# One head's reciprocal and scaling, moved to earlier places in VectorE's program

## The chip, the cores and the metric

The kernel runs on one core of a Trainium2 chip. The metric is the device time of one execution in microseconds (us). Engines are called PE (TensorE, matmuls), DVE (VectorE), ACT (ScalarE), POOL (GpSimd) and SP (SyncE, which here only issues DMAs). Each engine works through its own program in order, and they meet at semaphores.

## The reference

Two transformer-like layers over x of shape (4, 1024, 256). Layer 0 is a long convolution and an FFN with binarized weights; layer 1 is causal attention with 16 query heads on 4 key heads and a mixture-of-experts FFN. The change touches the attention alone:

```python
q = (hidden_states @ Wq).reshape(b, s, H, D).transpose(0, 2, 1, 3)      # H = 16, D = 64, s = 1024
k = (hidden_states @ Wk).reshape(b, s, HKV, D).transpose(0, 2, 1, 3)    # HKV = 4
v = (hidden_states @ Wv).reshape(b, s, HKV, D).transpose(0, 2, 1, 3)
q = _apply_rope(q, cos, sin)
k = _apply_rope(k, cos, sin)
scores = jnp.einsum('bkgqd,bkpd->bkgqp', qg, k) * scale
scores = jnp.where(causal, scores, jnp.float32(-1e+30))
probs = jax.nn.softmax(scores, axis=-1)
out = jnp.einsum('bkgqp,bkpd->bkgqd', probs, v).reshape(b, H, s, D)
return out.transpose(0, 2, 1, 3).reshape(b, s, H * D) @ Wo
```

The softmax of a head divides by a sum for each query. The kernel does this last: it multiplies the head's 64 x 1024 output by the inverse sums.

## The kernel before

A loop runs over the four batches. Inside it the layers follow each other; the attention is a loop over 16 heads (u, one "turn" each), and each turn over 12 blocks (n = 0 to 11) of the causal score matrix, 128 keys by up to 512 queries: 4 blocks for the first 512 queries, 8 for the second. The order of the work on each engine is written out by hand, and all that an engine does for a turn hangs on n:

- PE, block n: the scores of the block (`score_cols`), then score rows of the next head for its maxima (`score_rows`, one of 8 row tiles, at the n of `ROWS_AT`), at n = 8 the transposition of the maxima (`turn_maxima`), and the product with the values of the block four back (`values`). Scores go to six PSUM banks used in rotation. In turns 4 and 8 (and 0) PE also projects queries of a later key group at n = 4.
- ACT, block n: exp of the scores twice, to a full and a rounded copy (`exps`). Behind block 4 it copies out the second half of the previous head's output with its sums (`summed(u - 1, 1)`), behind block 8 the first half of this head's; behind block 9 it copies the next head's maxima (`turn_maxima`).
- POOL: masks of diagonal blocks, and the low part (full minus rounded) of blocks 0 to 5.
- DVE, block n: row maxima of the next head (`row_maxima`, tiles 0 and 1 at n = 0, then one tile for each n up to 6), their negation at n = 6 (`negate`), the low part of blocks 6 to 11 (`score_low`), and two small steps that finish an earlier head:
  - `invert(u)` waits for head u's sums in `den` and takes their reciprocals, 128 x 8, into `rden`;
  - `scale(u)` waits for the reciprocals spread over 64 partitions in `rb` (a part of the tile `mix`) and multiplies `osum` (in the tile `work`) by them into `oT`, 64 x 1024.
- SP, turn u, in this order: queries for later heads; `load_sums(u - 1)` (`den` from `osum`, issued once ACT has copied the sums); `load_maxima(u + 1)` (issued once ACT has copied the maxima); `spread_inverse(u - 1)`, which waits for the reciprocals, stores them to memory, waits for the store and loads them as a broadcast into `rb`; and in turns 0, 4, 8 the store of rotated rows to `q_scratch`, with a second one a turn later.

SP's part of a turn reads:

```python
                    if u:
                        load_sums(u - 1)
                    if u + 1 < HEADS:
                        load_maxima(u + 1)
                    if u:
                        spread_inverse(u - 1)
```

PE's first scores of a turn wait for the maxima that `load_maxima` brings, and ACT overwrites a head's half of `osum` two turns later, once its scaling is done.

Of the kernel before, what the change touches and what calls it, by code (L numbers as in the profile page):

```python
# [35 lines left out]
HEADS, KV, HD = 16, 4, 64  # L36
# [59 lines left out]
def adaln_hyena_binffn_gqa_moe(nc, d, out, gate_scratch, kf_scratch, q_scratch, k_scratch, inverse_scratch, scratch):  # L96
    es = ExitStack()
    with es:
# [792 lines left out]
        def _(dve):  # L891
# [131 lines left out]
            def rotate(k):  # L1023

                cols = slice(0, HALF) if (k % 2 if k >= 4 else k // 2) == 0 else slice(HALF, L)
                for e in range(2):
                    b = bk.wait(dve, ("rope", k, e))
                    V.tensor_tensor(turned(k)[:, 2 * e:2 * e + 2, :], ps[:, b, :].unsqueeze(1).broadcast_to([P, 2, HALF]),
                                    rope[:, :, cols], ALU.mult).then_inc(s["rope_a"], 1)
# [9 lines left out]
            def low(k):  # L1039

                dve.wait_ge(s["rope_hi"], k + 1)
                V.tensor_tensor(split_of(k)[:, 1], turned(k)[:, 0:2, :], split_of(k)[:, 0].bitcast(F32), ALU.subtract)\
                    .then_inc(s["rope_lo"], 1)

            def row_maxima(u, i):
                n = (i + 1) * P
                b = bk.wait(dve, ("rows", u, i))
                v = (ps[:, b:b + 2, :].rearrange("p a n -> p (a n)") if n > HALF else ps[:, b, :])[:, 0:n]
                V.tensor_tensor_reduce(out=v, in0=v, in1=mrow[:, L - n:L], scale=1.0, scalar=-3e38, op0=ALU.add,  # L1049
                                       op1=ALU.max, accum_out=mx[:, u % 2, i:i + 1]).then_inc(freed[b], 1)  # L1050

            def negate(u):
                dve.drain()
                V.tensor_scalar(nm[:, u % 2, :], mx[:, u % 2, :], -1.0, None, ALU.mult).then_inc(s["nm_done"], 1)
# [11 lines left out]
            def score_low(u, c, j):  # L1066
                if j * P >= c * HALF:
                    dve.wait_ge(s["masked_done"], NT * u + j + 1)
                else:
                    dve.wait_ge(s["exp_done"], NBLK * u + 4 * c + j + 1)  # L1070
                n, m = NBLK * u + 4 * c + j, HALF - max(0, j * P - c * HALF)
                V.tensor_tensor(plo[:, n % PRING, 0:m], full(n)[:, 0:m], phi[:, n % PRING, 0:m].bitcast(F32), ALU.subtract)\  # L1072
                    .then_inc(s["low_dve"], 1)

            def invert(u):
                dve.wait_ge(s["sum_loaded"], 16 * (u + 1))
                if u >= 2:
                    dve.wait_ge(s["inverse_stored"], 16 * (u - 1))
                V.reciprocal(rden[:, u % 2, :], den[:, u % 2, :]).then_inc(s["inverse_done"], 1)

            def scale(u):
                dve.wait_ge(s["inverse_loaded"], 16 * (u + 1))
                V.tensor_tensor(oT[u % 2 * HD:(u % 2 + 1) * HD, u // 2, :], osum[0:HD, u % 2, :], rb[:, :], ALU.mult)\
                    .then_inc(s["oT_done"], 1)
# [12 lines left out]
            with dve.Fori(0, B) as bi:  # L1097
# [3 lines left out]
                for n, e in enumerate(E_ORDER):  # L1101
                    dst = tapped(e)
                    b = bk.wait(dve, ("up", n, 1)) - 1
                    u = ps[:, b:b + 2, :].rearrange("p a n -> p (a n)")
# [91 lines left out]
                for u in range(HEADS):  # L1196
                    w = u + 1
                    k = 2 * GROUP_AT[u] + 2 if u in GROUP_AT else None
                    for n, blk in enumerate(BLOCKS):
                        if n == 4 and k and u:  # L1200
                            rotate(k)
                            rotate(k + 1)
                        if w < HEADS:
                            for i in ROWS_AT.get(n, ()):
                                row_maxima(w, i)
                        if n == 9 and u:
                            invert(u - 1)
                        if n == 6 and w < HEADS:
                            if w >= 2:
                                dve.wait_ge(s["nmr_done"], w - 1)  # L1210
                            negate(w)
                        if n == 7 and k:
                            low(k)
                        if blk in DVE_LOW:
                            score_low(u, *blk)
                        if n == 2 and u >= 2:
                            scale(u - 2)
                    if k:
                        low(k + 1)
                scale(HEADS - 2)  # L1220
                invert(HEADS - 1)
                scale(HEADS - 1)
                add_to_x("out1", 0, gates[:, 2, :])
# [410 lines left out]
```

## Time and profile before

| | |
|---|---|
| median of 3 runs | 2246.38 us (2244.85 to 2249.71) |
| the profiled execution | 2244.85 us, span in the profile 2243.0 us |
| busy over the span | PE 81%, DVE 68%, ACT 44%, POOL 47% |
| mean granted PE clock | 0.92 |
| attention turns of the first batch, 256 to 550 us | of 294 us: PE busy 248.58, DVE 195.34, ACT 183.23, POOL 201.09 |
| DVE's waits for the broadcast reciprocals | 53.3 us in 24 places |
| PE's waits for the maxima of a turn | 37.7 us in 56 places |

Busy times are those of an engine's own instructions; the rest of a line is idle. Times within the execution are counted from the start of the span. The share of busy time says little here; what counts is which wait ends last at each step of a turn.

### The profile page before, as it was taken

To read this page: it belongs to the slowest core of one execution; us is meant where nothing else is said; L and a number is where in the kernel's file an instruction comes from. 1 tells how busy PE (TensorE), PEld (TensorE's weight loads), DVE (VectorE), ACT (ScalarE), POOL (GpSimd) and SP (SyncE) were. 2 spreads that over 40 slices of the span, in tenths; PEclk is the share of its full clock that TensorE was granted. 3 is DMA by queue.
4 is the path that set the end of the run, shared out by engine and by line. 5 is a ranking of instruction groups with operands and counts; after the bars stand their busy time and mean duration, and the time that the engine had idled before them with its cause. 6 is when DMAs were issued, how large, how long until landed. Compare 5 with 4: busy or idle time off the path is not lost.

```text
span 2243.0 us, 27366 instructions
## 1 busy us (share of the span) xinstructions
PE 1808.7 (81%) x8596; PEld 1379.2 (61%) x8596; DVE 1533.7 (68%) x2838; ACT 996.5 (44%) x2113; POOL 1057.9 (47%) x1699
## 2 busy tenths in 40 slices
PE   6868788888866888878876878888887687978897
PEld 4657565566755666656665765665576475656666
DVE  4597866665668867666458886666555887766745
ACT  1303365565322345656331336556722043665643
POOL 0151366675133147667315127677722413766741
PEclk9989899999988889999988889999998898999999
DMA  5400433331410134332150043343141005333304
GB/s 223 178 1 1 113 102 97 90 88 33 169 49 1 49 98 108 91 95 67 30 202 1 1 113 90 78 109 89 35 174 54 1 1 146 90 95 81 85 25 188
DMA packets 92203, 187.26 MB, mean 83 GB/s; under 512 B 29119, under 2 KB 44287, under 8 KB 88326
## 3 DMA queue, kind: packets, MB, share of 16 engines
q1 hardware_dynamic: 84742, 171.66, 26.3%
q10 hardware_dynamic: 7296, 13.63, 2.1%
q8 instruction: 76, 1.25, 0.2%
q14 instruction: 89, 0.73, 0.1%
HBM read 129.39 MB, written 45.89 MB: 78 GB/s over the span
## 4 chain that ended last, share of the span: by engine, by line
PE 39%; DVE 16%; POOL 13%; DMA 10%; issue 8%; ACT 6%; DVEq 5%; SPq 1%; POOLq 1%; ACTq 0%
PE ps L367 7%; POOL plo L1316 6%; PE ps L663 5%; PE ps L490 5%; DMA q<-nmr 4%; PE ps L373 3%; DVE ps L1049 3%; DMA q_scratch<-hrow 3%; ACT phi L785 3%; PE ps L704 3%; PE ps L528 3%; PE ps L510 3%; PE ps L529 3%; PE ps L531 3%; POOL pT L1307 2%
## 5 line engine op out<-in xcount | busy, mean ns | idle before, releaser
L1049 DVE CUSTOM_DVE_ANT_0 ps<-ps,mrow 128x128 f32<-128x128 f32 (+7 forms) x512 | 384.0, 772 | 161.0 <-PE ps L490 160.7
L784 ACT ACTIVATE pT<-ps 128x512 f32<-128x512 f32 (+3 forms) x512 | 257.6, 503 | 286.8 <-POOL plo L1316 146.4
L785 ACT ACTIVATE phi<-ps 128x512 fp32r<-128x512 f32 (+3 forms) x768 | 377.6, 492 | 0.0
L1305 POOL TENSOR_SCALAR_AFFINE_SELECT phi<-phi 128x128 fp32r<-128x128 f32 x512 | 174.3, 340 | 404.9 <-ACT phi L785 400.5
L490 PE MATMUL ps<-khl,qhh 128*128 128x512 f32 (+3 forms) x768 | 241.5, 388 | 130.0 <-ACT phi L785 100.8
L510 PE MATMUL ps<-qhh,khl 128*128 128x512 f32 (+3 forms) x768 | 280.4, 365 | 50.6 <-DMA q<-nmr 37.7
L1316 POOL TENSOR_TENSOR plo<-pT,phi 128x512 fp32r<-128x512 f32 (+2 forms) x256 | 272.5, 1075 | 16.0
L511 PE MATMUL ps<-q,k 65*128 65x512 f32 (+3 forms) x768 | 272.1, 354 | 0.0
L528 PE MATMUL ps<-phi,vhi 128*65 128x512 f32 (+3 forms) x768 | 267.7, 349 | 2.0 <-POOL pT L1307 1.8
L531 PE MATMUL ps<-plo,vhi 128*65 128x512 f32 (+3 forms) x768 | 265.4, 346 | 4.2 <-POOL plo L1316 3.0
L529 PE MATMUL ps<-phi,vlo 128*65 128x512 f32 (+3 forms) x768 | 263.9, 344 | 0.0
L490 PEld LDWEIGHTS ps<-khl,qhh 128*128 128x128 f32 x768 | 139.9, 207 | 192.3 <-ACT phi L785 137.8
L1271 POOL TENSOR_TENSOR rstd<-var,neghalf 128x4 f32<-128x4 f32 x34 | 34.5, 1015 | 432.4 <-DVE var L961 432.4
L510 PEld LDWEIGHTS ps<-qhh,khl 128*128 128x128 f32 x768 | 149.5, 195 | 129.6 <-ACT phi L785 49.1
L1072 DVE TENSOR_TENSOR plo<-pT,phi 128x512 fp32r<-128x512 f32 (+2 forms) x256 | 156.3, 627 | 93.3 <-POOL pT L1307 64.5
L743 ACT ACTIVATE work<-ps,modb 128x512 f32<-128x512 f32 x48 | 37.3, 777 | 401.4 <-PE ps L445 401.4
L511 PEld LDWEIGHTS ps<-q,k 65*128 65x128 f32 x768 | 149.6, 195 | 12.6
L784 ACT ACTIVATE mix<-ps 128x512 f32<-128x512 f32 (+2 forms) x256 | 120.3, 470 | 60.3 <-PE ps L511 43.8
L531 PEld LDWEIGHTS ps<-plo,vhi 128*65 128x65 f32 x768 | 107.3, 140 | 57.6 <-POOL plo L1316 10.6
L367 PE MATMUL ps<-hT,wqkv 128*128 128x512 f32 x480 | 126.1, 422 | 18.9 <-DVE hT L973 18.9
L1316 POOL TENSOR_TENSOR plo<-mix,phi 128x256 fp32r<-128x256 f32 (+1 forms) x128 | 129.0, 1008 | 10.3 <-ACT phi L785 4.9
L1307 POOL TENSOR_SCALAR_AFFINE_SELECT pT<-pT 128x128 f32<-128x128 f32 x320 | 130.3, 407 | 0.0
(177 smaller groups left out, 3520.6 us busy)
## 6 DMA issues: line engine op xcount, KB each, us to landing
qhh<-q_scratch SPq DMA_DIRECT2D x112, 256.0 KB, 5.1
q_scratch<-hrow SPq DMA_DIRECT2D x24, 1024.0 KB, 5.5
mix<-inverse_scratch SPq DMA_DIRECT2D x64, 256.0 KB, 3.5
q<-q_scratch SPq DMA_DIRECT2D x56, 256.0 KB, 4.4
sgn<-sgn_scratch SPq DMA_DIRECT2D x8, 1024.0 KB, 13.6
Kf<-kf_scratch SPq DMA_DIRECT2D x4, 2048.0 KB, 17.3
khl<-k_scratch SPq DMA_DIRECT2D x24, 256.0 KB, 5.9
in_w<-in_w_scratch SPq DMA_DIRECT2D x4, 1536.0 KB, 10.8
```

The source lines that it names most:

```text
L367: i = mm(o, lhs(a, q), rhs(c, q), start=n == 0, stop=n == len(pairs) - 1)
L490: q = mm(ps[:, b + c // HALF, 0:e - c], qhh[:, r, i * P:(i + 1) * P], khl[:, g % 2, c:e], start=True, stop=True)
L510: mm(ps[:, b, 0:hi - lo], khl[:, g % 2, j * P:(j + 1) * P], qhh[:, r, lo:hi], start=True, stop=False)
L511: mm(ps[:, b, 0:hi - lo], k2[:, g % 2, j * P:(j + 1) * P], q2[:, u % 2, lo:hi], start=False, stop=True)\
L528: mm(o, vhi[:, g, j, :], high, start=j == 0, stop=False)
L529: mm(o, vlo[:, g, j, :], high, start=False, stop=False)
L531: mm(o, vhi[:, g, j, :], low, start=False, stop=j == 4 * c + 3).then_inc(s["pv_done"], 1)
L784: A(full(n)[:, 0:hi - lo], ps[:, b, 0:hi - lo], ACT.Exp, scale=SCALE)
L785: A(phi[:, n % PRING, 0:hi - lo], ps[:, b, 0:hi - lo], ACT.Exp, scale=SCALE)\
L1049: V.tensor_tensor_reduce(out=v, in0=v, in1=mrow[:, L - n:L], scale=1.0, scalar=-3e38, op0=ALU.add, op1=ALU.max, accum_out=mx[:, u % 2, i:i ...
L1307: G.affine_select(out=v, in_=v, compare_op=ALU.is_ge, fill=0.0, base=0, pattern=[[1, P]], channel_multiplier=-1).then_inc(s["masked_done"], 1)
L1316: G.tensor_tensor(plo[:, n % PRING, 0:m], full(n)[:, 0:m], phi[:, n % PRING, 0:m].bitcast(F32), ALU.subtract)\
```

## The change

In turn u, DVE takes the reciprocals of head u - 1 at block 4 instead of block 9, in front of the low parts, and scales head u - 1 at block 9 of the same turn, behind block 9's low part. Before, it scaled head u - 2 at block 2 of turn u. Head 14's scaling, which stood behind the loop, is thereby inside it. Nothing else is changed: the other engines' programs, SP's among them, are the same.

```diff
@@ -1203,7 +1203,7 @@
                         if w < HEADS:
                             for i in ROWS_AT.get(n, ()):
                                 row_maxima(w, i)
-                        if n == 9 and u:
+                        if n == 4 and u:
                             invert(u - 1)
                         if n == 6 and w < HEADS:
                             if w >= 2:
@@ -1213,11 +1213,10 @@
                             low(k)
                         if blk in DVE_LOW:
                             score_low(u, *blk)
-                        if n == 2 and u >= 2:
-                            scale(u - 2)
+                        if n == 9 and u:
+                            scale(u - 1)
                     if k:
                         low(k + 1)
-                scale(HEADS - 2)
                 invert(HEADS - 1)
                 scale(HEADS - 1)
                 add_to_x("out1", 0, gates[:, 2, :])
```

## Rows read from the trace of the kernel before

**Rows 1.** Windows: length, busy us (instructions) PE, PEld, DVE, ACT, POOL, clock, DMA.

```profile
392.15:408.23 16.08, 14.08 (x74) 9.84 (x74) 11.06 (x26) 11.05 (x27) 11.67 (x23) 1.00 0.30 67
...
356.00:358.00 2.00, 0.00 (x0) 0.00 (x0) 0.00 (x0) 0.00 (x0) 0.00 (x0) 1.00 1.05 394
...
360.00:362.00 2.00, 0.07 (x1) 0.07 (x1) 1.06 (x1) 2.00 (x4) 0.05 (x1) 0.50 0.93 199
```

**Rows 2.** Timeline of SP, heads 6 and 7: start us, us, engine line op out<-in.

```profile
390.20 0.69 SPq L1484 DMA_DIRECT2D q<-nmr  x1
390.93 0.44 SPq L1496 DMA_DIRECT2D inverse_scratch<-rden  x1
392.45 0.49 SPq L1500 DMA_DIRECT2D mix<-inverse_scratch  x1
...
400.28 0.52 SPq L1490 DMA_DIRECT2D den<-work  x1
406.28 0.69 SPq L1484 DMA_DIRECT2D q<-nmr  x1
```

**Rows 3.** Timeline of DVE, head 7; in brackets the idle time before.

```profile
390.70 0.56 DVE L1072 TENSOR_TENSOR plo<-pT,phi 128x384 fp32r<-128x384 f32 x1 [0.40 <-POOL pT L1307]
...
396.12 1.22 DVE L1083 TENSOR_TENSOR oT<-work,mix 64x1024 f32<-64x1024 f32 x1
...
400.54 1.10 DVE L1049 CUSTOM_DVE_ANT_0 ps<-ps,mrow 128x896 f32<-128x896 f32 x1 [1.41 <-PE ps L490]
...
406.18 0.20 DVE L1079 RECIPROCAL rden<-den 128x8 f32<-128x8 f32 x1
```

**Rows 4.** Timeline of PE, head 7: blocks 4 and 7, and the transposition.

```profile
396.19 0.45 PE L510 MATMUL ps<-qhh,khl 128*128 128x512 f32 x1
...
402.20 0.39 PE L510 MATMUL ps<-qhh,khl 128*128 128x512 f32 x1
...
403.75 0.27 PE L497 MATMUL ps<-ident,nm 128*8 128x128 f32 x1 [0.22 <-DVE nm L1054]
```

**Rows 5.** Timeline of ACT, head 7: block 4, the sums, the maxima.

```profile
398.69 0.60 ACT L784 ACTIVATE pT<-ps 128x512 f32<-128x512 f32 x1 [2.18 <-POOL plo L1316]
...
399.66 0.59 ACT L792 ACTIVATE work<-ps 65x512 f32<-65x512 f32 x1
...
406.00 0.25 ACT L771 ACTIVATE nmr<-ps 8x128 fp32r<-8x128 f32 x1
```

**Rows 6.** Tile `den`: landing of all 64 loads, from their issue.

```profile
DMA to landing us min/median/max: 2.0/2.7/4.7
```

**Rows 7.** Tile `mix`, 256 to 556 us: landing of SP's 16 broadcast loads.

```profile
DMA to landing us min/median/max: 3.3/3.5/4.0
```

**Rows 8.** Windows of DVE alone: length, busy us (instructions), clock, DMA share, GB/s.

```profile
391.60:392.70 1.10, 0.78 (x2) 1.00 0.07 4
392.90:394.95 2.05, 1.35 (x6) 1.00 0.58 160
```

**Rows 9.** Timeline of POOL, head 7: the second mask of block 1, block 3's.

```profile
396.15 1.35 POOL L1307 TENSOR_SCALAR_AFFINE_SELECT pT<-pT 128x128 f32<-128x128 f32 x1
...
400.07 0.29 POOL L1307 TENSOR_SCALAR_AFFINE_SELECT pT<-pT 128x128 f32<-128x128 f32 x1
```

**Rows 10.** The critical path behind head 4's turn: start us, us, what.

```profile
351.92 1.39 DMA inverse_scratch<-rden
...
353.86 5.91 DMA q_scratch<-hrow
```

**Rows 11.** Timeline of SP, heads 4 and 15.

```profile
350.17 0.69 SPq L1484 DMA_DIRECT2D q<-nmr  x1
...
541.35 0.51 SPq L1490 DMA_DIRECT2D den<-work  x1
```

**Rows 12.** Timeline of DVE, head 15: the low part of its last block.

```profile
549.01 0.29 DVE L1072 TENSOR_TENSOR plo<-mix,phi 128x128 fp32r<-128x128 f32 x1 [0.19 <-POOL mix L1307]
```

**Rows 13.** The critical path behind head 15's turn.

```profile
549.63 20.54 PE ps L663 x94
```

## The prediction

> **What bounds the kernel now.** I read the page first: the span is 2243.0 us. The critical path and PE's waits then put the disputed code in the attention part, which is 16 turns (one per head) in each of four batches. I took one ordinary turn, head u = 7, from its first score matmul at 392.15 us to the next turn's at 408.23, and laid the engines' timelines side by side. In those 16.08 us PE is busy 14.08, DVE 11.06, ACT 11.05 and POOL 11.67, with PE's clock granted in full [rows 1]. No engine is full. The turn is a loop of dependences, and the question is what the moved waits do to that loop.
>
> With blocks 0 to 11 of a turn, the loop is as follows. SP sends the row maxima of the next head (390.20); the first score matmul follows at 392.15. The exp of block 4 starts at 398.69, the maximum of row tile 6 runs at 400.54, the score matmul of block 7 is at 402.20 and the turning of the maxima at 403.75, ACT copies them out at 406.00, and SP sends the next ones at 406.28 [rows 2, 3, 4, 5]. 390.20 to 406.28 is the 16.08 us again.
>
> The slack around this loop is small. Block 7's score matmul takes the PSUM bank of tile 6, whose maximum ends at 400.54 + 1.10 = 401.64, 0.56 us before the matmul starts. Block 4's score matmul (396.19) has its bank from row tile 2. The exp of block 4 waits 2.18 us for POOL, so that matmul has slack: its first half takes 0.45 us and its second about as much less an overlap, so it ends near 396.9, and could end 1.8 us later for nothing [rows 3, 4, 5].
>
> **The reciprocal, moved from block 9 to block 4.** It needs the sums that SP loads. SP can issue this load only after ACT has copied the sums, which comes right behind block 4's exp: the copy starts at 399.66 and the load is issued at 400.28 [rows 2, 5]. Landing takes 2.7 us from issue in the median of 64, 2.0 to 4.7 at the ends [rows 6]. So the sums are there at 400.28 + 2.7 = 402.98. In the old order DVE reaches the reciprocal at 406.18 and doesn't wait. In the new order it reaches it behind tile 5's maximum, at 400.54 less the 1.41 us of idle time ahead of tile 6, 399.13, and everything behind it waits until 402.98, plus 0.2 for the reciprocal less 0.1 of overlap: 403.1. Behind it stand the maxima of tiles 6 and 7, the negation, and the low parts of blocks 6 to 11. Tile 6 starts at 403.1 instead of 400.54, so block 7's score matmul can't start before about 404.25 instead of 402.20. That is 2.56 us less the 0.56 of slack, and I take 2.1 (by the negation, whose slack is smaller, it is 2.2). From the exp of block 7 to the copy of the maxima ACT works without a pause, so the next SP send is late by the same 2.1 us. Nothing takes this back later in the loop.
>
> SP gains nothing from the earlier reciprocal in an ordinary turn. Its queue holds the send of the maxima (406.28) ahead of the store of the reciprocals, which goes right behind it (390.20 and 390.93); the reciprocal, at 406.18 in this turn, is in time for that already [rows 2, 3].
>
> **The scaling, moved from block 2 two turns behind the head's own to block 9 one turn behind.** Its factors come by a store (SP waits for its landing, from 390.93 to 392.45: 1.5 us) [rows 2] and a broadcast load (3.5 us in the median, 3.3 to 4.0) [rows 7]. The load is issued at 392.45, so the factors land at 395.95 [rows 2, 7], wherever the scaling stands in DVE's program; today the scaling starts at 396.12. In the new order DVE comes to it behind block 9's low part, which ends at 390.70 + 0.56 = 391.26. It then waits 4.7 us. Behind it now stand the low parts of blocks 10 and 11 and the maxima of tiles 0 to 3, which used that time before [rows 3, 8]. From 395.95: scaling 1.22, the two low parts 0.78, the maxima of tiles 0 to 2 with their read-outs 1.35 [rows 3, 8], less some 0.35 for overlaps (my estimate: each instruction starts up to 0.1 before the last one's end, and the last read-out needn't be waited for). That is 3.0, so tile 2's bank is free near 398.95, and block 4's score matmul goes from 396.19 to 399.0, 2.8 us later. On the way PE waits for block 10's low part. Its own exp moves from 398.69 to about 399.7: of the 2.8 us, 1.8 are covered by what it waited for POOL, and 1.0 us is left. The sums are then copied 1.0 us later, and the second wait stands behind them: 1.0 + 2.1 = 3.1 us per turn.
>
> One row makes the scaling cost more than its 1.22 us today: a mask of POOL takes 1.35 us beside it at 396.15 instead of 0.29, which lies on the loop [rows 9]. In the new order the scaling starts at the same moment, so this 1.06 us stays. The Trainium skill (SBUF — State Buffer, Who interferes with whom) has a DVE instruction with two SBUF inputs and a GpSimd instruction that reads SBUF shut each other out, the first one keeping the read port to its end. By that rule the low parts of blocks 10 and 11, which now run right behind the scaling, may hold POOL up to 0.8 us longer; that would fit in what the exp of block 4 waits for PE by then, and changes no term.
>
> **Turns that differ.** Heads 4 and 8 carry the projection of a later group at block 4 on PE. There the reciprocal stands behind four rotations on DVE and its sums have landed, so the first wait costs nothing. The projection sits directly behind block 4's score matmul, so here all 2.8 us pass. In return the reciprocal is no longer late. In these turns SP waits for it: the store at 351.92 has its trigger there, and the store of the rotated rows behind it, at 353.86 and 5.91 us long, is on the critical path [rows 10]. The earlier reciprocal lets SP go on right behind its send (350.17, and 0.73 as in the ordinary turn: 350.90), 1.0 us sooner [rows 2, 11]. Net 1.8 us per such turn. After heads 4 and 8 ACT stands still for that 5.91 us, so DVE's wait for the factors is hidden; heads 5 and 9, like head 1, pay only the first wait.
>
> Head 15 has no maxima to find. The load of its predecessor's sums is issued at 541.35 [rows 11] and lands at about 544.05, before the low parts are urgent. Store, load and scaling then take 1.5 + 3.5 + 1.22 from 544.3, to about 550.4, and the low parts of blocks 10 and 11, now behind it, end near 551.1 instead of 549.01 + 0.29 = 549.30. That is 1.8 us on the last value matmuls [rows 12]. Taking one scaling out of the end saves nothing: PE goes into the output projection without a pause, and is still in it when the last scaling is done (its projection matmuls follow each other for 20.54 us) [rows 13].
>
> **The sum, per batch.** Heads 2, 3, 6, 7 and 10 to 14: 9 x 3.1 = 27.9. Heads 1, 5, 9: 3 x 2.1 = 6.3. Heads 4, 8: 2 x 1.8 = 3.6. End: 1.8. Together 39.6 us, times four batches 158. The profiled execution took 2244.85 us (1.5 below the median of 2246.38 of the three runs), so the forecast is 2403 us.
>
> The unknown prices are the two landings. If every load of sums took 2.0 us, 12 turns a batch would be 0.7 cheaper each: 34 us less, 2369. If each took 4.7, 2.0 dearer each, 96 us more, 2499; since the median is near the short end, I take the middle of 2.7 and 4.7 as a mean that could be, 48 us more, 2451, and with the factors at 4.0 the upper end is 2473. The load of factors at 3.3 instead of 3.5 saves 0.2 x 11 x 4 = 9 us, at 4.0 it costs 22.
>
> The Trainium skill (DMA: Bandwidth & Descriptors, Anatomy of one DMA — SWDGE (gpsimd) path) gives about 2.0 us for any transfer plus bytes over 436 GB/s, and puts nearly all of it on the receipt of the write. It speaks against the change, since a 4 KB load then isn't quick: my estimate by its figures is 2.0 us for the sums, which would give the 2369 above but for the factors' path (4.6 us for store and load, where the rows have 5.0).
>
> **The rivals.**
> - *Only one wait shows.* The 1.0 us that I let pass at block 4 rests on a cover of 1.8 us that I read from one turn. If DVE and PE catch up fully, 9 turns cost 2.1 instead of 3.1 and heads 4 and 8 about nothing: 12 x 2.1 + 1.8 = 27 a batch, 2353 us. For it: DVE idles 16.08 - 11.06 = 5 us in a turn [rows 1]. Against it: that idle time is spread over waits for PE and POOL, and a chain that is late arrives late at each of them. Chance 0.14.
> - *Faster: the factors are there in time.* If SP had stored and loaded them before DVE comes to block 9, the scaling would run in a hole of DVE and would no longer stretch POOL's mask, which is on the loop: 1.06 us x 13 turns x 4 = 55 us less, 2190 us. It decides at one point: the factors must land before 391.3. For it: the reciprocal is ready 5 us earlier. Against it: SP's send of the maxima stands ahead of the store and goes at 390.20 [rows 2]. Chance 0.05.
> - *No change*, the waits all lying beside POOL's work: 2245 us. It needs 2.5 us of slack at tile 6, and the rows show 0.56. Chance 0.04.
> - *More: PE's clock.* PE gets holes of about 2.3 us (at block 10) and 2 us (before block 7) in a turn. The granted clock was full in this turn; should it fall to its lower level (1.2 GHz instead of 2.4) for some 4 us of each turn, and half of the doubled matmul time lie on the loop, that is 1 us x 15 x 4 = 60 us more, 2463 us, up to twice that. Against it: behind head 4's turn PE does nothing from 356 to 358 us at full clock, and only later, at 360 to 362, is it at 0.50 [rows 1]. Chance 0.09.
>
> **How the numbers follow.** The forecast as worked out has 0.68; its own range is 2360 (both short) to 2473. With the first rival's 0.14 the range reaches down to 2345, and with half of the clock's up to 2480. Faster by over 0.2% (about what a measurement of this kernel tells from no change) 0.05, within it 0.04, slower 0.91.
>
> **What would show it.** In the new profile: the scaling preceded by about 4.7 us of idle DVE, released by the load of the factors; a wait of 2.6 to 3.9 us before the reciprocal, put down to the load of the sums; SP's sends of the maxima 19.2 us apart in ordinary turns instead of 16.08; about 2 us of PE waiting for a row maximum before block 7's score. The mask of POOL beside the scaling should still take over 1 us. I am wrong if the sends stay near 16 us apart, if the load of the sums is issued before block 4's exp, or if the clock differs.

## The result, and the profile after

The changed kernel takes 2454.32 us in the median of 4 runs (2449.18 to 2458.99), the kernel before 2245.61 on the same chip: a ratio of 1.0925, 95% interval 1.0899 to 1.0953. It is slower by 209 us, where 158 were forecast. The profiled execution took 2463.96 us with a span of 2462.2, 219 above that of before.

These are the busy times on the two pages, the kernel before first. DVE, ACT and POOL are busy for less time than before or for as long. PE is busy for 116 us more with the same 8596 matmuls: its mean granted clock is 0.88 (0.92 before). In the first batch the attention of the changed kernel runs from about 256 to 612 us at a clock of 0.88; in the kernel before it ran from 256 to 550 us at 0.96.

```profile
PE 1808.7 (81%) x8596; PEld 1379.2 (61%) x8596; DVE 1533.7 (68%) x2838; ACT 996.5 (44%) x2113; POOL 1057.9 (47%) x1699
PE 1925.0 (78%) x8596; PEld 1467.6 (60%) x8596; DVE 1505.9 (61%) x2838; ACT 995.2 (40%) x2113; POOL 998.3 (41%) x1699
```

Read the waits next. These are rows of the changed kernel's waits (engine, line, releaser, us in total, times, longest).

```profile
DVE oT L1083 <- DMA mix<-inverse_scratch: 272.7, 62, 5.5
ACT pT L784 <- DVE plo L1072: 186.3, 48, 4.5
DVE rden L1079 <- DMA den<-work: 163.2, 56, 6.2
...
PE ps L531 <- DVE plo L1072: 115.4, 52, 2.9
...
PE ps L510 <- DVE mx L1049: 44.0, 34, 2.2
```

The first and third are the two waits of the change: 4.4 us each in 62 places, 2.9 us each in 56. The second is a surprise: ACT, 48 times, waits for a low part that DVE makes. Waits add up to more than the loss, because several engines wait for one thing. The chain says which of them set the end. Here it is for one whole ordinary turn of the changed kernel, head 7, from one send of the maxima to the next (start us, us, what):

```profile
411.88 0.69 SPq L1483
...
412.61 1.50 DMA inverse_scratch<-rden
414.13 3.61 DMA mix<-inverse_scratch
417.76 1.22 DVE oT L1083
...
419.01 0.44 DVE plo L1072
...
419.94 0.49 ACT phi L785
...
420.49 0.29 POOL phi L1304
420.79 0.26 POOL pT L1306
...
421.12 1.02 POOL plo L1315
...
422.24 0.60 ACT pT L784
...
423.33 0.49 ACT work L792
423.83 1.96 DMA den<-work
425.82 0.20 DVE rden L1079
...
427.12 0.50 PE ps L510
...
429.73 0.43 PE ps L531
...
431.70 0.15 ACT nmr L771
431.86 0.69 SPq L1483
```

The turn takes 431.86 - 411.88 = 19.98 us instead of 16.08 [rows 2]. For its first 5.8 us nothing computes on the chain: the send, the store, the broadcast load. Then come the scaling, block 10's low part, block 1's exp and its work on POOL, and block 4's exp; the copy of the sums, their load, the reciprocal, and block 7's scores behind tile 6's maximum.

DVE's timeline of the changed kernel has the same in its own rows, with the idle time ahead in brackets:

```profile
417.76 1.22 DVE L1083 TENSOR_TENSOR oT<-work,mix 64x1024 f32<-64x1024 f32 x1 [4.84 <-DMA mix<-inverse_scratch]
419.01 0.43 DVE L1072 TENSOR_TENSOR plo<-pT,phi 128x256 fp32r<-128x256 f32 x1
...
425.82 0.20 DVE L1079 RECIPROCAL rden<-den 128x8 f32<-128x8 f32 x1 [2.61 <-DMA den<-work]
425.94 1.07 DVE L1049 CUSTOM_DVE_ANT_0 ps<-ps,mrow 128x896 f32<-128x896 f32 x1
```

The scaling waits 4.84 us, the reciprocal 2.61. Windows of the changed kernel, with the columns of [rows 1], show the clock behind the second hole of PE: 0.74, then 0.50.

```profile
428.00:430.00 2.00, 1.89 (x8) 0.99 (x8) 1.62 (x5) 2.00 (x5) 0.00 (x0) 0.74 0.02 4
430.00:432.00 2.00, 2.00 (x7) 1.41 (x6) 0.69 (x1) 1.43 (x4) 0.77 (x3) 0.50 0.00 0
```

A good ruler for all kernels here is the time between SP's sends of the maxima, read from the start times in SP's timeline. The first batch (turns 0 to 14; "next" is from the last send to the next batch's first):

```text
turn                 0     1     2     3     4     5     6     7     8     9    10    11    12    13    14   next
before           21.79 19.41 16.03 15.88 20.12 24.00 16.03 16.08 20.10 23.94 16.20 16.07 16.01 16.07 16.34 264.51
after            21.79 21.56 20.60 20.39 24.71 24.23 20.75 19.98 26.13 25.77 20.19 20.09 21.58 19.75 21.38 267.46
e1_scale_only    21.78 20.42 17.58 19.23 25.96 23.29 19.22 20.20 26.07 23.24 18.82 20.56 20.09 20.36 20.80 272.91
e8 (e1, filled)  21.81 19.43 17.80 20.18 25.01 23.27 17.68 17.85 23.18 23.38 17.83 18.00 18.17 17.86 18.06 273.24
e2_invert_only   21.78 21.33 21.50 18.78 20.15 24.42 22.02 17.53 20.11 26.17 21.23 17.77 19.84 17.74 19.72 262.63
e6_spread_first  21.79 23.65 17.71 17.91 20.13 20.64 18.39 17.15 20.24 20.92 17.35 16.52 17.94 16.50 17.00 262.43
e7_both_free     21.78 19.99 15.44 15.26 20.28 20.42 15.48 15.28 22.79 19.66 16.03 17.10 15.27 15.26 15.69 263.84
```

Over four batches the mean difference of after and before is, for turns 2, 3, 6, 7 and 10 to 14, 39.1 us together (4.3 each); for 4 and 8, 5.2 and 5.9; for 1, 5 and 9, 1.9, -0.2 and 0.5; for the rest of a batch 2.3. That is 54.7 us a batch, 219 in four: the whole loss of the profiled execution.

### The profile page after: what moved, and what is told of

Same layout as the page of the kernel before. It is cut to its first block, busy times and chain, and to the rows that moved or that the text cites. A ratio compares the mean times of both kernels' runs of the same rounds, so it can differ in the third digit from the quotient of the medians.

```text
span 2462.2 us, 27366 instructions
## 1 busy us (share of the span) xinstructions
PE 1925.0 (78%) x8596; PEld 1467.6 (60%) x8596; DVE 1505.9 (61%) x2838; ACT 995.2 (40%) x2113; POOL 998.3 (41%) x1699
## 4 chain that ended last, share of the span: by engine, by line
PE 35%; DMA 21%; DVE 17%; issue 6%; ACT 6%; DVEq 5%; POOL 5%; SPq 2%; ACTq 1%; POOLq 1%
DMA mix<-inverse_scratch 8%; PE ps L367 6%; PE ps L663 5%; DMA den<-work 5%; DMA inverse_scratch<-rden 4%; PE ps L510 3%; PE ps L490 3%; PE ps L373 3%; DMA q_scratch<-hrow 3%; PE ps L511 3%; ACT phi L785 2%; PE ps L531 2%; PE ps L704 2%; DVE oT L1083 2%; PE ps L528 2%
## 5 line engine op out<-in xcount | busy, mean ns | idle before, releaser
L531 PE MATMUL ps<-plo,vhi 128*65 128x512 f32 (+3 forms) x768 | 283.4, 369 | 115.8 <-DVE plo L1072 115.4
L510 PE MATMUL ps<-qhh,khl 128*128 128x512 f32 (+3 forms) x768 | 307.1, 400 | 82.1 <-DVE mx L1049 44.0
L490 PE MATMUL ps<-khl,qhh 128*128 128x512 f32 (+3 forms) x768 | 258.8, 414 | 99.8 <-ACT phi L785 67.8
L511 PE MATMUL ps<-q,k 65*128 65x512 f32 (+3 forms) x768 | 292.7, 381 | 0.0
L528 PE MATMUL ps<-phi,vhi 128*65 128x512 f32 (+3 forms) x768 | 286.0, 372 | 0.0
L529 PE MATMUL ps<-phi,vlo 128*65 128x512 f32 (+3 forms) x768 | 280.8, 366 | 0.0
L1315 POOL TENSOR_TENSOR plo<-pT,phi 128x512 fp32r<-128x512 f32 (+2 forms) x256 | 255.3, 1008 | 16.0
L490 PEld LDWEIGHTS ps<-khl,qhh 128*128 128x128 f32 x768 | 161.5, 229 | 154.7 <-ACT phi L785 81.9
L1083 DVE TENSOR_TENSOR oT<-work,mix 64x1024 f32<-64x1024 f32 x64 | 78.9, 1233 | 272.9 <-DMA mix<-inverse_scratch 272.7
L511 PEld LDWEIGHTS ps<-q,k 65*128 65x128 f32 x768 | 164.1, 214 | 17.4
## 6 DMA issues: line engine op xcount, KB each, us to landing
Kf<-kf_scratch SPq DMA_DIRECT2D x4, 2048.0 KB, 17.6
```

Of the source, the lines that this page charges most:

```text
L490: q = mm(ps[:, b + c // HALF, 0:e - c], qhh[:, r, i * P:(i + 1) * P], khl[:, g % 2, c:e], start=True, stop=True)
L510: mm(ps[:, b, 0:hi - lo], khl[:, g % 2, j * P:(j + 1) * P], qhh[:, r, lo:hi], start=True, stop=False)
L511: mm(ps[:, b, 0:hi - lo], k2[:, g % 2, j * P:(j + 1) * P], q2[:, u % 2, lo:hi], start=False, stop=True)\
L528: mm(o, vhi[:, g, j, :], high, start=j == 0, stop=False)
L529: mm(o, vlo[:, g, j, :], high, start=False, stop=False)
L531: mm(o, vhi[:, g, j, :], low, start=False, stop=j == 4 * c + 3).then_inc(s["pv_done"], 1)
```

## The experiments

Times are medians; ratios are to the kernel before, run beside, with a 95% interval. The diffs are against the changed kernel unless said.

**Each part alone.** The two moves were made one at a time. e1_scale_only leaves the reciprocal at block 9:

```diff
-                        if n == 4 and u:
+                        if n == 9 and u:
                             invert(u - 1)
```

> The scaling alone stands in its new place (block 9 of the next turn); the reciprocal stays at block 9, in front of it. Theory A (read from the changed kernel's trace): the wait for the factors also holds the low part of block 10, and ACT's exp of block 1 waits for that low part because its full-precision copies have three places; some 1.9 us per ordinary turn, some 4 to 5 in the turns of heads 4 and 8 (the projection follows at a lower clock), 2 at the end: about 29 us a batch, 2362 us. Theory B (as forecast): only the PSUM banks of the row maxima pass the wait on: 9 x 1.0 + 2 x 2.8 + 1.8 = 16.4 us a batch, 2311 us.

Measured: 2452.56 us, 1.0913 (1.0893 to 1.0932). Both expectations are far too low; one wait alone costs as much as both together. Its ordinary turns, in the table, differ in length, and the granted clock goes with it: in the first batch head 2's 17.58 us are at 1.00, the turns of 18.8 to 19.2 us at 0.91, and those of 20.1 to 20.8 us at 0.83 or 0.84. Windows of this kernel show it: head 2's whole turn, then three stretches of head 7's.

```profile
300.75:318.33 17.58, 14.48 (x75) 10.04 (x73) 10.50 (x26) 10.86 (x28) 10.49 (x23) 1.00 0.41 120
414.00:416.00 2.00, 2.00 (x8) 1.54 (x9) 1.97 (x10) 1.76 (x6) 0.99 (x3) 0.50 0.11 23
416.00:418.00 2.00, 2.00 (x7) 1.55 (x7) 0.96 (x3) 0.80 (x2) 1.92 (x5) 0.50 0.00 0
418.00:420.00 2.00, 2.00 (x6) 1.48 (x5) 0.87 (x2) 0.79 (x3) 1.92 (x4) 0.50 0.00 0
```

Where the clock stays full the wait passes on 1.6 us (17.58 against 16.03). Where it falls behind PE's hole for block 10's low part, to the lower of its two levels (1.2 GHz), PE becomes the chain: matmuls of 512 columns start 0.43 us apart instead of 0.23, and the turn takes 18.8 to 20.8 us. In head 7's turn three of them start at 417.81, 418.23 and 418.66, on a chain that runs over PE without a break from 413.92 to 421.97.

e2_invert_only leaves the scaling where it was before, and moves the reciprocal:

```diff
-                        if n == 9 and u:
-                            scale(u - 1)
+                        if n == 2 and u >= 2:
+                            scale(u - 2)
                     if k:
                         low(k + 1)
+                scale(HEADS - 2)
```

> The reciprocal alone stands in its new place (block 4); the scaling stays at block 2, two turns behind. Both theories: 12 turns a batch wait for the sums before tile 6's maximum, 2.1 us each if the sums land in 2.7 us as before the change, less 1 us in each of two turns: about 23 us a batch, 2339 us. If the sums land in 2.0 us, as after the change: 1.4 each, 15 us a batch, 2306 us. If the two waits are independent, this and the scaling alone add up to the whole change (209 us).

Measured: 2371.48 us, 1.0544 (1.0524 to 1.0564), above both figures expected. Turn 7 pays 1.5 us and turns 4 and 8 nothing, as forecast for 4 and 8. But heads 2, 6 and 10 pay 5 to 6 us. SP's timeline of this kernel shows why in head 2's turn:

```profile
303.52 0.60 SPq L1460 DMA_DIRECT2D q_scratch<-hrow  x1
309.14 0.53 SPq L1479 DMA_DIRECT2D q<-q_scratch  x1
309.72 1.24 SPq L1474 DMA_DIRECT2D qhh<-q_scratch  x2
311.00 0.60 SPq L1490 DMA_DIRECT2D den<-work  x1
```

The load of the sums stands behind query loads that wait for the store of rotated rows, and the reciprocal follows at 315.21, after 5.43 us of idle DVE. The landing of the sums is 2.6 us in this kernel's median and 5.0 at most.

The parts cost 2452.56 - 2248.76 = 204 and 2371.48 - 2248.76 = 123 us, 327 together, and the whole change costs 209. The prices don't add. The profiled executions differ by 110 us in the same way, and the turns' means over the batches say where: 45 us lie in heads 2, 6 and 10, where e2 pays 16.2 us a batch by itself, 38 in the other ordinary turns, and 22 behind the last send of a batch. The last are another matter than holes: there e1 pays 8.4 us and the changed kernel 2.3, because e1 takes head 14's reciprocal at block 9 (593.98 us) and waits 5.07 us for its factors before the scaling, where the changed kernel took it at block 4 (600.87) and waits 0.16. For the 45 and the 38 the runs don't settle the cause.

**The clock, taken out.** e8_scale_only_fill is e1 with seven redundant repeats of row tile 3's score-row matmul, right behind it and ahead of PE's wait for block 10's low part, in 11 turns of a batch; the output stays the same. Against e1:

```diff
+FILL = {(u, 3): 7 for u in (2, 3, 4, 6, 7, 8, 10, 11, 12, 13, 14)}
...
+                for _ in range(FILL.get((u - 1, i), 0)):
                     q = mm(ps[:, b + c // HALF, 0:e - c], qhh[:, r, i * P:(i + 1) * P], khl[:, g % 2, c:e],
                            start=True, stop=True)
```

> The kernel with the scaling alone moved, with row tile 3's matmul repeated 7 times (1.5 us) in PE's hole of 2.8 us in 11 turns a batch; the output is the same. If PE's lower clock behind that hole makes the difference between its turns of 17.6 us (granted clock 1.00) and of 20.2 us: the turns come down to 17.6 to 18.0 us and those of heads 4 and 8 by 2.5, 2365 to 2375 us instead of 2453. If the lower clock is only a sign of the wait and costs nothing: 2453 us.

Measured: 2381.68 us, 1.0604 (1.0579 to 1.0629), 71 us below e1 although PE has more to do, and near the 2365 to 2375 expected. The wait for the factors is nearly as long (293.0 us in 64 places, 300.1 in e1). The clock of the first batch's attention is 0.94 instead of 0.87, and all ordinary turns of that batch but head 3's are at 1.00 and take 17.6 to 18.2 us. The same window of both kernels, e1 first:

```profile
256.00:612.00 356.00, 285.64 (x1274) 209.16 (x1273) 193.56 (x403) 183.37 (x441) 185.29 (x364) 0.87 0.28 70
256.00:612.00 356.00, 303.56 (x1449) 222.63 (x1449) 202.38 (x430) 184.44 (x444) 186.97 (x365) 0.94 0.27 69
```

So at least 71 of e1's 204 us are the lower clock behind the hole.

e4_fill does it to the full change: seven repeats in the same place, and four of row tile 7's matmul, behind it and ahead of the wait for tile 6's maximum, in nine turns.

```diff
+FILL = {**{(u, 3): 7 for u in (2, 3, 4, 6, 7, 8, 10, 11, 12, 13, 14)},
+         **{(u, 7): 4 for u in (2, 3, 6, 7, 10, 11, 12, 13, 14)}}
```

> The changed kernel with redundant matmuls in PE's holes: row tile 3's matmul repeated 7 times (1.5 us) ahead of the wait for block 10's low part in 11 turns, tile 7's second half repeated 4 times (0.9 us) ahead of the wait for tile 6's maximum in 9 turns; the output is the same. Theory A with the clock: the granted clock of the attention turns (0.88) rises to 0.95 or more and the turns get shorter by about 1 us, 40 us in all, 2414 us. If the lower clock costs nothing: 2454 us or a few more, whatever the clock does. If the holes aren't what lowers the clock, it stays at 0.88.

Measured: 2437.35 us, 1.084 (1.0821 to 1.0859), with 0.95 for the attention's clock. The clock rose as expected, but only 17 us come back instead of 40, most of it in turns 4 and 8 (23.1 to 23.5 us against 25.7). The ordinary turns still take 20.3 us in the mean (20.4 unfilled), although 27 of the 36 ran at 0.98 or more, where none of the changed kernel's was above 0.94. The repeats cost PE time too, so 17 is a lower bound of the clock's share in the full change; the upper one stays open, and that the clock lengthens the ordinary turns of the full change is not shown.

**Where the scaling stands.** e3_scale_at_11 puts it behind blocks 10 and 11:

```diff
-                        if n == 9 and u:
+                        if n == 11 and u:
                             scale(u - 1)
```

> The changed kernel with the scaling behind block 11's low part instead of behind block 9's, so that no low part stands behind the wait. Theory A: the exp of block 1 isn't held, block 4's exp is late by 0.6 us instead of 1.9, and POOL's mask beside the scaling takes over 1 us again; heads 4 and 8 gain 0.8, the end 1.8: about 60 us less than the change, 2394 us, and ACT's wait of 3.9 us before block 1 is gone. Theory B: 0.75 us less in 11 turns and 1.8 at the end, 40 us less, 2414 us. If the waits in front of the low parts cost nothing: 2454 us.

Measured: 2416.53 us, 1.0756 (1.0733 to 1.078). It tests the new row of the waits, of which nothing is left for this exp. In ACT's timeline of this kernel block 1's exp no longer waits for DVE:

```profile
483.05 0.49 ACT L784 ACTIVATE pT<-ps 128x384 f32<-128x384 f32 x1 [0.19 <-PE ps L511]
```

In the changed kernel ACT waited 3.88 us before the same exp (head 7), put down to DVE's low part. Three full-precision copies are used in rotation, so block 1's exp needs block 10's low part done. Taking that away gives 38 us; the wait for the factors still blocks the row maxima, and 168 us of loss stay. The time is the one that theory B gave (2414), not theory A's 2394. Yet A's signs are there: block 4's exp in head 7's turn starts 9.13 us behind the send (10.36 in the changed kernel, 8.49 before), and POOL's longest mask of an ordinary turn takes 0.97 us in the mean again (0.30 in the changed kernel, 0.96 before). The wait was real, but putting block 10 first saved less than A's price for it.

e5_scale_at_tile5 puts the old scaling, in the kernel before, somewhere else without a wait, to ask what its stretched mask was worth:

```diff
+                        if n == 4 and u >= 2:
+                            scale(u - 2)
                         if n == 9 and u:
                             invert(u - 1)
...
-                        if n == 2 and u >= 2:
-                            scale(u - 2)
```

> The kernel before, with its scaling (two turns behind) moved from block 2 to block 4, behind tile 5's maximum, where DVE idles 1.4 us. If the 1.06 us by which the scaling stretches POOL's mask at block 1 lie on the loop of a turn, this gives back up to 1.06 us in 12 turns a batch, less what the scaling now holds up on POOL behind block 4: 2200 to 2225 us. If that mask isn't on the loop: 2246 us.

Measured: 2237.19 us, 0.9954 (0.9934 to 0.9973), where 2200 to 2225 were expected. Ordinary turns take 15.74 instead of 16.05 us, and heads 4 and 8 lose 0.75. The 1.06 us didn't vanish, it moved. POOL's timeline of this kernel:

```profile
401.98 1.28 POOL L1305 TENSOR_SCALAR_AFFINE_SELECT phi<-phi 128x128 fp32r<-128x128 f32 x1
```

and DVE's:

```profile
401.53 1.57 DVE L1083 TENSOR_TENSOR oT<-work,mix 64x1024 f32<-64x1024 f32 x1
...
405.58 0.98 DVE L1054 TENSOR_SCALAR nm<-mx 128x8 f32<-128x8 f32 x1
```

Another mask takes 1.28 us beside the scaling, and the negation of the maxima, 0.17 us in the changed kernel, takes 0.98 beside POOL's low part. The Trainium skill (SBUF — State Buffer, Who interferes with whom) says that a DVE instruction with two SBUF inputs, or one of a kind such as tensor_scalar in its two-port mode, and a GpSimd instruction that reads SBUF block each other in the order of issue; both rows agree, though none shows in which mode the negation ran.

**The order on SP.** The rival "faster" hung on one condition: the factors must land before DVE comes to the scaling. e6_spread_first meets it by putting the store and broadcast ahead of the send, which the earlier reciprocal allows:

```diff
-                    if u + 1 < HEADS:
-                        load_maxima(u + 1)
                     if u:
                         spread_inverse(u - 1)
+                    if u + 1 < HEADS:
+                        load_maxima(u + 1)
```

> The changed kernel, with SP's store and load of the reciprocals ahead of its send of the next head's maxima. Theory A: the factors land before DVE comes to block 9, the wait before the scaling is gone and what hangs on it (low part of block 10, exp of block 1, PE's hole), POOL's mask is no longer stretched; the wait for the sums at block 4 stays, and the time comes near the reciprocal alone (2371) less 1 us in 11 turns, 2320 to 2330 us. The forecast's count: 2190 + 100 for the sums, 2290 us. If SP, waiting for the reciprocal, holds up the send of the maxima: 2400 us or more.

Measured: 2278.87 us, 1.0148 (1.0124 to 1.0173). 175 of the 209 us are back by this one swap, more than theory A or the forecast's count gave. The scaling's wait is gone but for eight places (21.4 us in all), and turns 5 and 9, where the store of rotated rows now goes out sooner, fall from about 24 to between 20.6 and 22.1 us. What is left is the wait for the sums: 2.9 us ahead of tile 6 in the turn of head 7.

e7_both_free adds to it a place for the reciprocal behind the negation, and for the scaling behind block 11:

```diff
-                        if n == 4 and u:
-                            invert(u - 1)
...
+                        if n == 6 and u:
+                            invert(u - 1)
...
-                        if n == 9 and u:
+                        if n == 11 and u:
                             scale(u - 1)
```

> As the last one, and the reciprocal stands at block 6 behind the negation of the maxima, the scaling behind block 11's low part. Theory A: no maximum stands behind the wait for the sums, the factors land about when DVE comes to the scaling, the mask of POOL isn't stretched (1.06 us in 12 turns a batch) and SP comes to the store of the rotated rows 3 us sooner in the turns of heads 4 and 8; less 3 to 4 us a batch in the three turns where the sums land in over 4 us: 2180 to 2205 us, faster than the kernel before. If the reciprocal in front of block 6's low part or SP's order holds up the send of the maxima by 1 us in each turn: 2250 us or more.

Measured: 2206.22 us, 0.9816 (0.9796 to 0.9837): faster than both kernels, 41 us under the kernel before (2247.64 beside it). SP's timeline of this kernel in head 7's turn:

```profile
398.58 0.52 SPq L1489 DMA_DIRECT2D den<-work  x1
402.06 0.33 SPq L1495 DMA_DIRECT2D inverse_scratch<-rden  x1
404.08 0.47 SPq L1499 DMA_DIRECT2D mix<-inverse_scratch  x1
404.59 0.70 SPq L1483 DMA_DIRECT2D q<-nmr  x1
```

and DVE's:

```profile
401.82 0.20 DVE L1079 RECIPROCAL rden<-den 128x8 f32<-128x8 f32 x1
...
407.78 1.22 DVE L1083 TENSOR_TENSOR oT<-work,mix 64x1024 f32<-64x1024 f32 x1 [0.75 <-DMA mix<-inverse_scratch]
```

The reciprocal doesn't wait. The factors land about when DVE is at the end of the turn (the scaling waits 0.75 us here, and in 21 of 64 places in all), and the mask of POOL that stood beside the old scaling takes 0.29 us again (at 395.48). Most ordinary turns take 15.2 to 15.7 us instead of 16.05, turns 5 and 9 some 20 instead of 24. Turns 8 and 11 (22.8 and 17.1, and much the same in most later batches) show what is not free yet: the send now stands behind the broadcast, and PE starts turn 8 at 407.66, 3.07 us behind it, after 1.74 us of waiting, with the clock at 0.50 behind (409 to 411).

Two more kernels split that result. e9_order_alone is the kernel before with the swap on SP and nothing else.

> The kernel before with SP's order alone turned: store and broadcast of the reciprocals ahead of the send of the maxima, DVE's program as it was. It asks whether the 2206 us of the kernel with both waits free come from SP's order by itself. Theory A: no. In the old DVE order the reciprocal is ready at 406.18 in head 7's turn, at the same time as the maxima, so the send waits for the store and its landing, 1.5 us, and for the issue of the broadcast, 0.5: about 2.0 us later in each of some 12 ordinary turns, 24 us a batch, 2340 us; scalings then wait less or the same. Theory B: SP's order is itself the gain (the store of rotated rows gets out sooner): about 2206 us. Between them, if the send had 2 us of slack: 2245.

Measured: 2450.08 us, 1.0908 (1.0888 to 1.0929). The swap is ruinous without the earlier reciprocal. Theory A has the sign right, and the size wrong again: ordinary turns take 20.3 us, 4.2 more, not 2.0. SP's timeline of this kernel:

```profile
414.56 0.32 SPq L1496 DMA_DIRECT2D inverse_scratch<-rden  x1
415.96 0.47 SPq L1500 DMA_DIRECT2D mix<-inverse_scratch  x1
416.47 0.69 SPq L1484 DMA_DIRECT2D q<-nmr  x1
```

and PE's at the start of the next turn:

```profile
419.60 0.77 PE L510 MATMUL ps<-qhh,khl 128*128 128x512 f32 x1 [3.88 <-DMA q<-nmr]
```

The send is issued 2.1 us behind the reciprocal (414.33) and PE starts 3.13 us behind the send, where it was 1.95 before (406.28 to 408.23): the small load is slower beside the broadcast. And behind the hole of 3.88 us the first matmul already takes 0.77 us instead of 0.47, and in the turn before PE ran at 0.50 from 400 to 404.

e10_sums_wait_only is e6 with the scaling at block 11, so that it differs from e7 by the reciprocal's place alone.

```diff
-                        if n == 9 and u:
+                        if n == 11 and u:
                             scale(u - 1)
```

> The kernel with the store ahead of the send, reciprocal still at block 4, scaling put at block 11 instead of 9. It differs from the kernel with both waits free (2206 us) by the place of the reciprocal alone, and from the one with the store first (2279) by the place of the scaling alone. Theory A: what is left in the 2279 is the wait for the sums, 2.9 us ahead of tile 6; the scaling's factors have landed when DVE reaches it at block 9, so its place costs only its own 1.2 us ahead of two low parts: 2255 to 2275 us, of the 72 us between them most belongs to the reciprocal. Theory B: the scaling's place is what costs, 1.2 us ahead of block 10's low part in each turn, with the wait for the sums covered: 1.2 x 13 x 4 = 62 us less, about 2215.

Measured: 2265.41 us, 1.0095 (1.0078 to 1.0112). Theory A holds. With the factors in time, the scaling's place is worth 13 us (2278.87 to 2265.41) and the wait for the sums 59 (2265.41 to 2206.22).

## Why the prediction came out as it did

**Right: the direction, and both waits.** SP's send goes right ahead of the store (411.88, 412.61) and the store and load take 1.50 and 3.61 us, so the factors land where they always did and the scaling waits 4.84 us for them (4.7 forecast). The reciprocal waits 2.61 for the sums (2.6 to 3.9 forecast). Undoing the first wait at its cause gave back 175 us, a later place for the scaling 13 more, and undoing the second wait 59 more. Of the signs named, the sends are further apart than the 19.2 us forecast (20.4 in the mean), and PE's wait before block 7's scores is shorter, 1.22 us in head 7 where about 2 were forecast.

**Partly luck: the time inside the range.** The forecast was 2403 us, and 2454 lies in the upper part of the range. That part was there for landings longer than 2.7 and 3.5 us and for the rival of the clock. The sums landed sooner than the forecast's 2.7 and the factors about as forecast, so what filled the range was mostly other terms, below: the cover at block 4, and heads 4 and 8.

**Mis-sized: the 1.0 us that block 4's exp was to pass on; it is 1.87.** From send to that exp the old kernel took 8.49 us (390.20 to 398.69 [rows 2, 5]), the new one 10.36 (411.88 to 422.24). The step that failed is "of the 2.8 us, 1.8 are covered by what it waited for POOL". That cover was no fixed date. POOL itself waits for block 1's exp, and this waits for block 10's low part, through the rotation of three copies. ACT's timeline of the kernel before has block 1's exp in head 7,

```profile
394.16 0.49 ACT L784 ACTIVATE pT<-ps 128x384 f32<-128x384 f32 x1 [0.18 <-PE ps L511]
394.55 0.48 ACT L785 ACTIVATE phi<-ps 128x384 fp32r<-128x384 f32 x1
```

and POOL's timeline of the kernel before the first mask on it:

```profile
395.90 0.29 POOL L1305 TENSOR_SCALAR_AFFINE_SELECT phi<-phi 128x128 fp32r<-128x128 f32 x1
```

The exp stood 3.96 us behind the send (394.16 - 390.20) and stands 7.67 behind it (419.55 - 411.88), 3.71 later. POOL gives back 0.87, which is how long that mask had waited behind POOL's earlier work (exp done at 394.55 + 0.48 = 395.03, mask at 395.90), and the 1.06 of the next point. 1.78 is left, near the 1.87. The path over PSUM banks, by which I priced it, was there too but ended sooner: block 4's score matmuls were done at 421.80, and its exp started at 422.24, put down to POOL. e3 shows the coupling: the wait goes when block 10 is put first, and 38 us with it, but the row maxima are then still late and hold most of the delay.

**Wrong: "this 1.06 us stays".** The mask takes 0.30 us in the new kernel (0.26 on its chain), since POOL comes to it only after the scaling. This error had the other sign and hid part of the first. e5 shows that such a stretch moves with the scaling rather than vanishing.

**Mis-sized: the reciprocal's 2.1 us; it is 1.4.** Block 7's scores come 15.24 us behind the send instead of 12.00, 3.24 later, of which 1.87 was there already. The sums landed in 2.0 us in the median (1.9 to 3.9), not 2.7. The old median stood for unlike turns: in the kernel before, the loads in the turns of heads 5, 7, 9, 11, 13 and 15 landed in 2.0 us (head 9's in up to 3.2), head 7's, the model turn, among them; those in the turns of heads 2, 6 and 10 took 4.0 to 4.7, and the rest mostly 2.5 to 4. Head 7's own load would have given the term of 1.4. In e2 the median is 2.6, and the turns of heads 2, 6 and 10, with 4.0 to 5.0, pay 5 to 6 us.

**Partly true: the rival of PE's clock, given 0.09.** From block 7's scores to the next send the turn loses another 0.66 us (3.90 in all), in the stretch at 0.74 and 0.50. 1.87 + 1.37 + 0.66 = 3.90 against 3.1. Against the rival I had set an idle stretch after which the clock was still full for a while; that row was no evidence for safety, for two us later it stood at 0.50. The last sign of being wrong that the prediction names, a clock that differs, did show: 0.96 fell to 0.88 in the first batch's attention. By e8 against e1 the clock is worth at least 71 us where only the scaling waits.

**Mis-sized: heads 4 and 8, 5.5 us instead of 1.8, and heads 5 and 9, 0.15 instead of 2.1.** In head 4's turn, with a projection, PE stands still for 2.31 us ahead of block 10's last product (349.83), and windows of the changed kernel show what follows, ahead of and under the first of the 24 matmuls of the projection (from 352.87):

```profile
350.00:352.00 2.00, 1.83 (x9) 1.42 (x8) 1.97 (x9) 1.66 (x6) 1.08 (x3) 0.61 1.04 229
352.00:354.00 2.00, 2.00 (x6) 1.60 (x6) 0.71 (x2) 0.89 (x2) 1.92 (x6) 0.53 0.93 209
354.00:356.00 2.00, 2.00 (x10) 1.61 (x9) 1.08 (x1) 0.67 (x2) 1.92 (x4) 1.00 0.03 5
```

Filling the hole (e4) brings these turns from 25.4 and 26.0 us in the mean down to 23.2 and 23.3, so 2.1 and 2.7 us of the 5.5 are the clock; the other 3 or so are near the 2.8 that I let pass. But I also credited the earlier store of rotated rows to heads 4 and 8, 1.0 us. It is there (the store of the rows 2.78 us behind the send at 366.90, before 3.69 [rows 10, 11]), but by the turns' lengths it counts one turn on, in heads 5 and 9: with the mask's 1.06 it would take nearly all of what these pay for the reciprocal. No run has it alone, but in e6, where that store goes out 0.7 us behind the send, heads 5 and 9 are 3.4 and 2.6 us shorter in the mean than in the kernel before. Head 1 (1.9 against 2.1) and the end (2.3 against 1.8) were near.

**The sum.** Per batch: 39.1 instead of 27.9 for the nine ordinary turns, 11.1 instead of 3.6, 2.2 instead of 6.3, 2.3 instead of 1.8. That is 54.7 against 39.6. I took the turn of head 7 for all nine, and it is one of the cheap ones (3.90; mean 4.3). The difference between them is not settled: they differ in how much of them ran at the lower clock, but e4, which raised it, left their mean length nearly as it was.

**The rival "faster" had the right condition.** It was met by no part of this change, and by one swap on SP it was (e6); with the reciprocal out of the way of tile 6 it became a gain (e7). The price I gave it, 55 us for the mask, was too high for that part alone: e5 gives 10 us for moving the scaling off that mask, onto another. That the swap alone costs 205 us (e9) shows that it needs the reciprocal's earlier place.

## What to carry to other kernels

When a wait is moved up in an engine's in-order program, price it by what stands behind the waiting instruction and by every ring that these instructions free for other engines; a wait seen on another engine covers the delay only if its releaser doesn't move with it. Ask first whether the thing waited for can come sooner: here its store stood behind another DMA on SP, and the same early reciprocal was worth a loss of 209 us or a gain of 41, by the order of two DMAs and by standing behind the urgent work instead of ahead of it. And treat new holes on the matmul engine as a cost of their own, to be tested by filling them (71 us in one kernel here, 17 in another). Don't add the prices of two moves that were measured one at a time: here 327 us stood against 209.

## What the runs showed of the hardware that was not expected

The granted PE clock fell to 0.50 behind idle stretches of PE of 2 to 3 us (2.56 us ahead of 413.92 in e1, head 7, then 0.50 from 414 to 420 us; 2.31 us in the changed kernel, head 4, then 0.61 and 0.53 from 350 to 354). Yet it stayed at 1.00 behind others of the same length (2.27 us in the changed kernel, head 7, then 1.00 from 420 to 428; 2.41 us in e1, head 2 of the third batch, 1.00 for the whole turn). Redundant matmuls in the hole, with nearly the same waits around them, made the kernel 71 us faster.

A load of 4 KB issued directly behind the 256 KB broadcast on the same queue let PE start 3.13 us after its issue (e9), against 1.95 without it. A negation of 128 x 8 took 0.98 us instead of 0.17 beside a POOL instruction (e5).
